# Attention weights as max(row factor, column factor) times the mask, column-grouped products in the third layer, three of its heads on GpSimd

## The chip, the cores and the metric

One core of a Trainium2 chip runs the whole program in one launch. The metric is the device time in microseconds (us) of that core, from launch to end. The engines work side by side, each through its own in-order list of instructions: TensorE (PE, its weight loads shown as PEld), VectorE (DVE), ScalarE (ACT), GpSimd (POOL), and SyncE (SP), which issues the DMAs. They meet only in semaphores. A matmul result lands in PSUM, which has eight banks of 128 x 512 fp32 here; GpSimd does not read PSUM in this kernel.

## The reference

16 graphs of 512 nodes with 128 features pass through four graph-attention layers, each with a residual and a layer norm over the features behind it. All graphs share one adjacency mask. Cut to the parts that matter:

```python
# layer 0: 4 heads, scores = q.k/sqrt(32), masked softmax, P @ v, output projection
# layer 1 (one head), layer 3b (second attention of layer 3), both with the mask:
h = x @ W;  s1 = h @ a1;  s2 = h @ a2
e = leaky_relu(s1[:, None] + s2[None, :], 0.2)          # N x N
out = softmax(where(adj > 0, e, -inf), -1) @ h
# layer 2: 8 heads of 16 features, same scores per head, plus beta*log(prior+eps), mask, softmax
# layer 3: relu(x @ mlp1) -> attention of 256 features without a mask -> elu, residual
#          -> relu(@ mlp2) -> attention of 128 features with the mask -> elu, residual
```

A score depends on one number of the row i and one of the column j. Up to a factor that depends on the row alone and cancels in the softmax, exp(leaky_relu(s + d)) is max(exp(d), exp(0.2 d) * exp(-0.8 s)), with d the target's and s the source's term.

## The kernel before, in words

The program is written out by hand as stages. `STAGES` (line 27) gives a letter to each stage of each engine and `ORDER` (line 47) is, for each engine, a string of pairs (letter, graph in hex): the exact order in which the engine issues its stages. It is software-pipelined: while graph 7 is in layer 0, graph 6 is in layer 1, graph 5 in layers 1 and 2 and graph 4 in layers 2 and 3. After about graph 3 the strings repeat with one period per graph. `BANK_OF_USE` (line 156) names the PSUM bank of every PE stage; `wrote(stage, g, k)` waits until PE has filled that use of a bank, `took` until its reader has emptied it, and `sig` waits on a named signal. P = 128 partitions, C = 4 chunks of 128 nodes; every weight matrix is held transposed, source j on the partitions (4 chunks) and target i along 512 columns. All of it is fp32 unless said. One fp32 matmul shows as two instructions, one fp32 transpose as one.

**Layer 0** (`l0_*`). Per graph: 16 score matmuls with 32 rows each, four of them on four row groups at once (L479); DVE adds the mask and takes the row maximum (L993); ACT takes the exponential (L731); PE transposes the 128 x 512 probabilities, 64 transposes (L487), ACT copies them back (L741); PE multiplies by v in four column groups of 32, 128 columns each (L498).

**Layers 1, 3 and 3b** (`gat`, names l1, l3, l3b). DVE computes dd, the target term less its maximum (L1077), ACT makes b = exp(dd) and g = exp(0.2 dd) (L766, L767). PE spreads the source term over all partitions with four transposes of a broadcast column (L545), DVE brings it to SBUF with a cap (L1087, tile R, 128 x 512), ACT exponentiates it there (L773), DVE makes P = max(R * g, b) in four instructions (L1100), and in l1 and l3b POOL multiplies each by the mask in place (L1309). PE multiplies P by [h, 1] (L556 for l1 and l3b, L640 for l3), which gives numerator and denominator.

**Layer 2** (l2). Instead of P it builds a 0/1 matrix per head. PE spreads the head's source term (`l2_s`, L580: 4 transposes a head, 8 heads), DVE compares it with -d and multiplies by the mask, 4 instructions a head, bf16 out (`l2_signs`, L1170, tile B, two buffers). POOL builds G, both branches of h times their target factors (L1337, L1339), ACT rounds it to bf16 (L804) and POOL splits the rest in two further bf16 pieces (L1347, L1350, L1355), so that three bf16 products (102 columns) carry the fp32 value. PE: `l2_v` (L592, 16 matmuls a head) and `l2_md` (L605, the unsplit mask times the second branch, 48 matmuls). ACT copies each product out (L810, tile EV, and L818, tile MD), POOL adds the three pieces (L1363, L1367, tile U) and combines the branches (L1386, L1374, L1388), DVE takes the reciprocal (L1179), POOL divides (L1396, tile O).

**Norms.** In each layer DVE takes the statistics (L1037, L1047), POOL the power -1/2 in four short instructions (L1279 to L1294), ACT applies it (L781). POOL also adds the output bias (L1271), the residual of layer 1 (L1303) and takes min(v, 0) for the elus (L1315).

## Time and profile before

| | |
|---|---|
| median of 3 runs | 1220.33 us (1213.86 to 1223.62) |
| the profiled execution's own time | 1216.26 us |
| its span in the profile | 1214.5 us |
| mean granted TensorE clock | 0.968 of 2.4 GHz |
| PE busy | 1077.1 us (89%) |
| PEld busy | 884.0 us (73%) |
| DVE busy | 969.3 us (80%) |
| ACT busy | 835.3 us (69%) |
| POOL busy | 730.7 us (60%) |

Page part 2, the span in 40 slices, a digit being tenths of busy time:

```profile
PE   2889989899999999999999999999999978788662
DVE  3467898978898889889889888898888887967432
ACT  1788788686878787878787787878787554534431
POOL 0024566566577575858667685758485869566412
PEclk9999999999999999999999999999999989979886
```

The first slice loads and prepares the weights; from the sixth on the strings repeat; the last six or seven are the drain, in which fewer and fewer graphs are left to overlap. A busy time of PE counts each matmul from its start to its modelled end, so consecutive matmuls overlap, and a gap shorter than that overlap does not show as idle. The spacing between the starts of two rows in the timeline shows what a run of instructions really takes.

### The profile page before, as it was taken

What the parts mean: (1) busy time and instruction counts of PE and PEld (TensorE: products, weight loads), DVE (VectorE), ACT (ScalarE), POOL (GpSimd) and SP (SyncE); (2) the same over time, 40 slices, a digit from 0 to 9 for tenths busy, and PEclk for the clock granted to TensorE, in tenths of its full rate; (3) what the DMA queues carried; (4) which work ended last, traced back from release to release, by engine and by line L of the source; (5) the groups of instructions that cost most, each with busy time, mean ns of one, the idle gap of its engine ahead of it and who ended that gap; (6) DMA issues with size and microseconds to landing.
All of it is one profiled execution on the core that took longest, in us unless ns stands there. A gap on an engine that the chain in (4) does not pass through costs nothing. (4 is left out here: it accounts for less than half of the span.)

```text
span 1214.5 us, 30981 instructions
## 1 busy us (share of the span) xinstructions
PE 1077.1 (89%) x10997; PEld 884.0 (73%) x10997; DVE 969.3 (80%) x2482; ACT 835.3 (69%) x2045; POOL 730.7 (60%) x991
## 2 busy tenths in 40 slices
PE   2889989899999999999999999999999978788662
PEld 1566868787878787787878888887878867667452
DVE  3467898978898889889889888898888887967432
ACT  1788788686878787878787787878787554534431
POOL 0024566566577575858667685758485869566412
PEclk9999999999999999999999999999999989979886
DMA  4000000000000000000000000000000000000000
GB/s 112 2 10 11 11 11 2 10 2 1 11 11 10 11 10 11 10 11 10 11 11 7 7 8 11 11 10 11 11 2 11 1 10 1 10 1 10 10 9 9
DMA packets 9510, 13.24 MB, mean 11 GB/s; under 512 B 2704, under 2 KB 5008, under 8 KB 9232
## 3 DMA queue, kind: packets, MB, share of 16 engines
q1 hardware_dynamic: 9360, 11.28, 3.0%
q8 instruction: 90, 1.47, 0.5%
q14 instruction: 60, 0.49, 0.1%
HBM read 7.08 MB, written 4.19 MB: 9 GB/s over the span
## 5 line engine op out<-in xcount | busy, mean ns | idle before, releaser
L1170 DVE SCALAR_TENSOR_TENSOR B<-bank,neg_d,mask_t 128x512 bf16<-128x512 f32 x512 | 346.7, 738 | 6.1 <-PE bank L580 6.1
L993 DVE CUSTOM_DVE_ANT_0 probs<-bank,mask_add 128x512 f32<-128x512 f32 x256 | 169.8, 682 | 47.7 <-PE bank L479 47.5
L731 ACT ACTIVATE probs<-probs,neg_max 128x512 f32<-128x512 f32 x256 | 183.2, 718 | 14.6 <-DVE neg_max L1001 14.6
L741 ACT ACTIVATE probs_t<-bank 128x512 f32<-128x512 f32 x256 | 148.5, 596 | 24.2 <-PE bank L487 21.2
L487 PE MATMUL bank<-ident,probs 128*128 128x128 f32 x1024 | 145.4, 277 | 16.6 <-ACT probs_t L741 7.7
L1363 POOL TENSOR_TENSOR U<-EV 128x136 f32<-128x136 f32 x128 | 57.8, 451 | 167.8 <-ACT EV L810 166.2
L487 PEld LDWEIGHTS bank<-ident,probs 128*128 128x128 f32 x1024 | 112.7, 141 | 38.7 <-ACT probs L731 19.6
L640 PE MATMUL bank<-t,l_P 128*128 128x257 f32 x512 | 123.8, 395 | 11.1 <-DVE l_P L1100 11.0
L592 PEld LDWEIGHTS bank<-GS,B 128*128 128x128 bf16 x2048 | 105.8, 98 | 24.6 <-issue 15.0
L640 PEld LDWEIGHTS bank<-t,l_P 128*128 128x128 f32 x512 | 96.8, 196 | 35.4 <-DVE l_P L1100 14.1
L592 PE MATMUL bank<-GS,B 128*128 128x102 bf16 x2048 | 115.0, 209 | 3.3 <-issue 2.0
L781 ACT ACTIVATE x<-x,shift_l,rstd_l 128x128 f32<-128x128 f32 x256 | 105.0, 482 | 17.0 <-POOL shift_l L1294 16.1
L1100 DVE TENSOR_SCALAR l_P<-l_R,l_g,l_b 128x512 f32<-128x512 f32 x128 | 102.8, 815 | 5.3 <-ACT l_R L773 2.3
L1309 POOL TENSOR_TENSOR l3b_P<-l3b_P,mask_t 128x512 f32<-128x512 f32 x64 | 75.3, 1182 | 48.6 <-DVE l3b_P L1100 48.6
L810 ACT ACTIVATE EV<-bank 128x408 f32<-128x408 f32 x128 | 64.7, 505 | 37.2 <-PE bank L592 34.1
L1309 POOL TENSOR_TENSOR l_P<-l_P,mask_t 128x512 f32<-128x512 f32 x64 | 76.5, 1201 | 21.8 <-DVE l_P L1100 21.8
L580 PE MATMUL bank<-ident,t 128*128 128x128 f32 x512 | 78.3, 282 | 0.0
L479 PE MATMUL bank<-head_k,head_q 32*128 32x512 f32 x512 | 72.7, 638 | 2.4 <-ACT probs_t L741 2.4
L556 PE MATMUL bank<-t,l3b_P 128*128 128x129 f32 x512 | 64.0, 280 | 7.3 <-POOL l3b_P L1309 7.3
L1287 POOL TENSOR_TENSOR rstd_l<-rstd_l,neg_half 128x4 f32<-128x4 f32 x64 | 68.5, 1070 | 3.0
L498 PE MATMUL bank<-probs_t,v 128*32 128x128 f32 x2048 | 69.2, 276 | 0.0
L1367 POOL TENSOR_TENSOR U<-U,EV 128x136 f32<-128x136 f32 x128 | 65.6, 516 | 5.8
(170 smaller groups left out, 2448.3 us busy)
## 6 DMA issues: line engine op xcount, KB each, us to landing
x_in<-in_x SPq DMA_DIRECT2D x16, 256.0 KB, 2.7
out<-x SPq DMA_DIRECT2D x16, 256.0 KB, 2.0
l_P<-in_adj SPq DMA_DIRECT2D x1, 1024.0 KB, 5.0
w_fc<-in_L_gnn_W_fc SPq DMA_DIRECT2D x1, 256.0 KB, 3.2
probs_t<-in_L_gnn_a_fc SPq DMA_DIRECT2D x1, 256.0 KB, 5.9
w_cat<-in_L_gnn_W SPq DMA_DIRECT2D x2, 64.0 KB, 3.4
w3a<-in_L_gnn_mlp_w SPq DMA_DIRECT2D x1, 128.0 KB, 3.4
w3b<-in_L_gnn_mlp_w SPq DMA_DIRECT2D x1, 128.0 KB, 3.1
```

The source lines that it names most:

```text
L479: pe.matmul(ps("l0_s", g, HEADS0 * c + h)[:, :], g.of(head_q)[rows, c * P:(c + 1) * P], g.of(head_k)[rows, :], start=True, stop=True)\
L487: last = pe.transpose(ps[:, j * P:(j + 1) * P], probs[m // HEADS0 % 2][:, m % HEADS0, j * P:(j + 1) * P], ident[:, :])
L580: last = pe.transpose(ps[:, c * P:(c + 1) * P], g.of(t2)[:, c, D + h:D + h + 1].broadcast_to([P, P]), ident[:, :])
L592: last = pe.matmul(ps[:, c * w3:(c + 1) * w3], B1[h % 2][:, j, c * P:(c + 1) * P], g.of(GS)[:, j * HEADS2 + h, :, :].rearrange("p a b -> p ...
L640: last = pe.matmul(ps[:, 0:HID + 1], gat["l3"]["P"][:, j, c * P:(c + 1) * P], g.of(t3)[:, j, 2:3 + HID], start=(j == 0), stop=(j == C - 1))
L731: act.activation(e, e, ACT.Exp, bias=neg_max[:, m:m + 1], scale=SCALE0, accum_out=g.of(den0)[:, m:m + 1])\
L741: act.activation(probs_t[c % 2][:, h, :, :].rearrange("p j n -> p (j n)"), ps("l0_t", g, m)[:, :], ACT.Copy)\
L781: last = act.activation(y[:, c, :], y[:, c, :], ACT.Identity, bias=shift[n][:, c:c + 1], scale=rstd[n][:, c:c + 1])
L993: dve.tensor_tensor_reduce(probs[c % 2][:, h, :], ps("l0_s", g, m)[:, :], mask_add[:, c, :], 1.0, -3.0e38, ALU.add, ALU.max, row_max[:, m: ...
L1100: dve.tensor_scalar(q["P"][:, j, :], q["R"][:, :], q["g"][:, j:j + 1], q["b"][:, j:j + 1], ALU.mult, ALU.max).then_inc(signal[n + "_P"], 1)
L1170: last = dve.scalar_tensor_tensor(B1[h % 2][:, j, :], ps("l2_s", g, h)[:, :], g.of(neg_d)[:, j, h:h + 1], mask_t[:, j, :], ALU.is_ge, ALU. ...
L1309: pool.tensor_tensor(t, t, mask_t[:, j, :], ALU.mult).then_inc(signal[n + "_Pm"], 1)
```

## The change

In all attention layers the exponential of the source term is taken on the 128 x 4 column before it is spread, not on the 128 x 512 tile after it, so DVE reads the spread factor straight from PSUM. In l1, l3b and l2 the common factor exp(0.2 d) moves from the weights into h (one POOL multiplication per layer), so a weight is max(spread factor, exp(0.8 d)) * mask, one `scalar_tensor_tensor` on DVE, with nothing for POOL to mask. Layer 2 keeps fp32 weights (P2, five slots of 128 x 4 x 512) and drops the bf16 pieces. Its products run in two groups of four heads: each head is one column group of 32 and streams 512 columns. ACT copies a group's 128 x 512 result out, PE transposes it back (`l2_n`), DVE divides (`l2_rcp`, `l2_o`). DVE makes the weights of heads 0 to 4; those of heads 5 to 7 are made by POOL: SP writes the three heads' factors to DRAM (`l2_rows`) and reads them back broadcast to all partitions (`l2_spread`, tile far_R), POOL takes the maximum in 12 instructions (`l2_p`) and multiplies by the mask in three of 128 x 2048 (`l2_m`). Heads 4, 6 and 7 reuse slots 0, 2 and 3 of the first group; head 5 has slot 4. t2 and t4 become single buffers. All order strings and the bank string are new.

```diff
 # SP (new)
+            def l2_rows(g, k):
+                sp.wait_ge(*sig("exp2", g, 3))
+                ...
+                sp.dma_start(g.of(rows2).rearrange("h p c -> p h c"), g.of(R2)[:, DVE_HEADS2:HEADS2, :])\
+                    .then_inc(signal["rows2"], 16)
+            def l2_spread(g, k):
+                sp.wait_ge(*sig("rows2", g, 16))
+                if g.has(1):
+                    sp.wait_ge(*sig("p2_max", g, 4 * FAR_HEADS2, back=1))
+                sp.dma_start(far_R[:, :, :, :].rearrange("q h p c -> q (h p c)"),
+                             g.of(rows2)....broadcast_to([P, FAR_HEADS2 * N_NODES])).then_inc(signal["spread2"], 16)
 # PE
             def attend(n, t):
-                        pe.wait_ge(*sig(n + "_Pm", g, 4))
+                        pe.wait_ge(*took(n + "_s", g))
+                        pe.wait_ge(*sig(n + "_gh", g, 1))
             def l2_s(g, h):
-                    last = pe.transpose(ps[:, c * P:(c + 1) * P], g.of(t2)[:, c, D + h:D + h + 1].broadcast_to([P, P]), ...)
+                    last = pe.transpose(ps[:, c * P:(c + 1) * P], g.of(R2)[:, h, c:c + 1].broadcast_to([P, P]), ident[:, :])
-            def l2_v(g, h):
-                for c in range(C):
-                    for j in range(C):
-                        last = pe.matmul(ps[:, c * w3:(c + 1) * w3], B1[h % 2][:, j, c * P:(c + 1) * P],
-                                         g.of(GS)[:, j * HEADS2 + h, :, :]...)
-            def l2_md(g, k):
-                ...
+            def l2_v(g, q):
+                if q == 0:
+                    pe.wait_ge(*sig("gh2", g, 1))
+                pe.wait_ge(*took("l2_s", g, GROUP2 * q + min(GROUP2, DVE_HEADS2 - GROUP2 * q) - 1))
+                if q == 1:
+                    pe.wait_ge(*sig("p2_far", g, FAR_HEADS2))
+                for j in range(C):
+                    for h in range(GROUP2):
+                        last = pe.matmul(ps[DH0 * h:DH0 * (h + 1), :], g.of(GH)[:, j, (GROUP2 * q + h) * W2:(GROUP2 * q + h) * W2 + DH0],
+                                         P2[:, slot_of(GROUP2 * q + h), j, :], start=(j == 0), stop=(j == C - 1))
+            def l2_n(g, q):
+                pe.wait_ge(*took("l2_v", g, q))
+                for c in range(C):
+                    last = pe.transpose(ps[:, c * P:(c + 1) * P], o2_raw[:, c * P:(c + 1) * P], ident[:, :])
 # ACT
-            def exp_sources(n): ...        # Exp on R, 128 x 512
-            def l2_high(g, k): ...         # G to bf16
+                    act.activation(t["R"][:, :], t["ss"][:, :], ACT.Exp, scale=-0.8)      # 128 x 4
+            def l2_v(g, q):
+                act.activation(o2_raw[:, :], ps("l2_v", g, q)[:, :], ACT.Copy)
 # DVE
-            def source_scores(n): ...      # R <- PSUM, 128 x 512
+            def masked_weights(n):         # l1, l3b; the wait on the spread bank and n_b is at j == 0
+                    made = dve.scalar_tensor_tensor(q["P"][:, j, :], ps(n + "_s", g)[:, :], q["b"][:, j:j + 1],
+                                                    mask_t[:, j, :], ALU.max, ALU.mult)
             def weights(n, last_part):     # l3
-                    dve.tensor_scalar(q["P"][:, j, :], q["R"][:, :], q["g"][:, j:j + 1], q["b"][:, j:j + 1], ...)
+                    made = dve.tensor_scalar(q["P"][:, j, :], ps(n + "_s", g)[:, :], q["g"][:, j:j + 1], q["b"][:, j:j + 1], ...)
-            def l2_signs(g, h): ...
+            def l2_p(g, h):                # heads 0 to 4
+                if h == 0:
+                    dve.wait_ge(*sig("exp2", g, 3))
+                    if g.has(1):
+                        dve.wait_ge(*wrote("l2_v", g, 1, back=1))
+                if h == GROUP2:
+                    dve.wait_ge(*wrote("l2_v", g, 0))
+                for j in range(C):
+                    last = dve.scalar_tensor_tensor(P2[:, h % GROUP2, j, :], ps("l2_s", g, h)[:, :], g.of(t2e)[:, j, h:h + 1],
+                                                    mask_t[:, j, :], ALU.max, ALU.mult)
+            def l2_rcp(g, q): ...          # reciprocal of 128 x 16 from PSUM
+            def l2_o(g, q): ...            # 128 x 256 from PSUM times the reciprocal
 # POOL
-            def mask_weights(n): ...       # l1, l3b
-            l2_g, l2_split, l2_u, l2_w, l2_c, l2_o
+            def scale(n, t): ...           # h * exp(0.2 d), 128 x 512, for l1 and l3b
+            def l2_scale(g, k): ...        # the same for layer 2
+            def l2_p(g, n):                # n = 0..11: head 5 + n // 4, chunk n % 4
+                if n == 0:
+                    pool.wait_ge(*sig("spread2", g, 16))
+                    if g.has(1):
+                        pool.wait_ge(*wrote("l2_v", g, 1, back=1))
+                if n == 4:
+                    pool.wait_ge(*wrote("l2_v", g, 0))
+                pool.tensor_scalar(P2[:, slot_of(DVE_HEADS2 + h), j, :].rearrange("q (c p) -> q c p", c=C),
+                                   far_R[:, h, :, :].rearrange("q p c -> q c p"), g.of(t2e)[:, j, ...], None, ALU.max)
+            def l2_m(g, h):
+                pool.wait_ge(*sig("p2_max", g, C * (h + 1)))
+                pool.tensor_tensor(p, p, mask_t[:, :, :], ALU.mult)       # 128 x 2048, fp32 times bf16
```

The part of the new strings that repeats with each graph, for the graph numbers of one period. POOL: `j5 b6 s3 c6 a8 d6 k5k5k5k5 p4 y5 q4 r4 e6 k5k5k5k5 y5 k5k5k5 t3 k5 f6 y5 g6 h6 i6 u3 v3 w3 x3`, where j is `l2_scale`, k `l2_p`, y `l2_m`, e and t the two `scale`, f the residual of layer 1. On PE the first product group of a graph (`t`) comes early in the period and the second late: `t5` D3 e7 D3 x4 m6 s5 f7 E3 f7 y4y4 F3F3 f7 n6 z4z4 G3 z4z4 n6 H3 f7 e8 f7f7 g7 A4 f7 J3J3 B4 f7 e8 u5 `t5`.

## Rows read from the trace of the kernel before

**Rows 1.** SP's timeline: start us, us, engine, what; two loads of x_in.
```profile
431.19 0.33 SPq L415 DMA_DIRECT2D x_in<-in_x  x1
497.59 0.33 SPq L415 DMA_DIRECT2D x_in<-in_x  x1
```

**Rows 2.** Windows, one period and the drain: length, then PE, PEld, DVE, ACT, POOL.
```profile
407.70:474.10 66.40, 64.54 (x690) 53.72 (x688) 58.98 (x154) 51.75 (x127) 45.75 (x62) 1.00 0.03 10
...
1040.00:1214.00 174.00, 115.91 (x760) 93.14 (x758) 94.95 (x215) 68.63 (x157) 80.67 (x107) 0.82 0.02 7
```

**Rows 3.** Groups by line, PE: count, then busy us, mean ns, idle before.
```profile
L487 PE MATMUL bank<-ident,probs 128*128 128x128 f32 x1024 | 145.4, 277 | 16.6 <-ACT probs_t L741 7.7 <-ACT probs L731 6.5 <-DVE v L980 1.8
L580 PE MATMUL bank<-ident,t 128*128 128x128 f32 x512 | 78.3, 282 | 0.0
```

**Rows 4.** PE's timeline, 600 to 611 us: start, us, line, operation, count.
```profile
600.27 0.88 PE L592 MATMUL bank<-GS,B 128*128 128x102 bf16 x16
600.99 1.49 PE L487 MATMUL bank<-ident,probs 128*128 128x128 f32 x12
...
603.96 0.89 PE L592 MATMUL bank<-GS,B 128*128 128x102 bf16 x16
604.78 1.14 PE L479 MATMUL bank<-head_k,head_q 32*128 32x512 f32 x8
605.86 1.75 PE L605 MATMUL bank<-GS,mask_t 128*128 128x136 bf16 x24
607.54 1.08 PE L498 MATMUL bank<-probs_t,v 128*32 128x128 f32 x32
608.43 1.06 PE L508 MATMUL bank<-ident,rden 128*32 128x128 f32 x32
...
610.02 1.04 PE L580 MATMUL bank<-ident,t 128*128 128x128 f32 x8
610.89 0.60 PE L450 MATMUL bank<-ident,x 128*128 128x128 f32 x4
```

**Rows 5.** Groups by line, DVE.
```profile
L1170 DVE SCALAR_TENSOR_TENSOR B<-bank,neg_d,mask_t 128x512 bf16<-128x512 f32 x512 | 346.7, 738 | 6.1 <-PE bank L580 6.1
...
L1100 DVE TENSOR_SCALAR l_P<-l_R,l_g,l_b 128x512 f32<-128x512 f32 x128 | 102.8, 815 | 5.3 <-ACT l_R L773 2.3 <-issue 2.2
...
L1100 DVE TENSOR_SCALAR l3b_P<-l3b_R,l3b_g,l3b_b 128x512 f32<-128x512 f32 x64 | 53.9, 851 | 2.3 <-ACT l3b_R L773 2.3
...
L1087 DVE TENSOR_SCALAR l_R<-bank,l_ndmax 128x512 f32<-128x512 f32 x32 | 23.9, 747 | 1.8 <-issue 1.7
```

**Rows 6.** Groups by line, ACT.
```profile
L741 ACT ACTIVATE probs_t<-bank 128x512 f32<-128x512 f32 x256 | 148.5, 596 | 24.2 <-PE bank L487 21.2
L810 ACT ACTIVATE EV<-bank 128x408 f32<-128x408 f32 x128 | 64.7, 505 | 37.2 <-PE bank L592 34.1 <-POOL U L1367 1.4
```

**Rows 7.** Groups by line, POOL.
```profile
L1309 POOL TENSOR_TENSOR l_P<-l_P,mask_t 128x512 f32<-128x512 f32 x64 | 76.5, 1201 | 21.8 <-DVE l_P L1100 21.8
...
L1315 POOL TENSOR_SCALAR e<-v 128x1024 f32<-128x1024 f32 x16 | 45.2, 2826 | 17.0 <-ACT v L846 16.8
...
L1347 POOL TENSOR_TENSOR G<-G,GS 128x1088 f32<-128x1088 f32 x16 | 40.6, 2540 | 16.0 <-ACT GS L804 16.0
L1337 POOL TENSOR_TENSOR G<-t,bg 128x512 f32<-128x512 f32 x32 | 33.9, 1058 | 11.6 <-ACT R L796 11.6
...
L1315 POOL TENSOR_SCALAR e<-x 128x512 f32<-128x512 f32 x16 | 23.9, 1491 | 30.1 <-issue 30.1
```

**Rows 8.** DMA issues: size, median us from issue to landing.
```profile
probs_t<-in_L_gnn_a_fc SPq DMA_DIRECT2D x1, 256.0 KB, 5.9
```

**Rows 9.** DVE's timeline near 305 us.
```profile
304.95 1.75 DVE L1001 TENSOR_SCALAR neg_max<-row_max 128x4 f32<-128x4 f32 x1
```

**Rows 10.** POOL's timeline at the same time.
```profile
304.57 2.11 POOL L1355 TENSOR_TENSOR GS<-G,GS 128x1088 bf16<-128x1088 f32 x1
```

**Rows 11.** PE's timeline in the last 20 us: the last masked attention.
```profile
1194.37 5.43 PE L556 MATMUL bank<-t,l3b_P 128*128 128x129 f32 x32 [7.30 <-POOL l3b_P L1309]
```

568 lines of the change are left out of this document (236 added, 332 removed), and 24 rows, old and new, of tables (STAGES, stored).

## The prediction, on record before the changed kernel ran

> **What bounds the kernel now.** I read the timeline of SP first, for the length of a period: two loads of x_in lie 497.59 - 431.19 = 66.4 us apart [rows 1]. Then the windows, for the load of each engine within one such period: PE 64.5 us, DVE 59.0, ACT 51.8, POOL 45.8 [rows 2]. So PE is the fullest and DVE is close behind. The reader should not take PE's 97% at its word. A row of transposes is 277 to 282 ns long [rows 3], while in an unbroken run the next one starts after 0.109 us (8 in 610.89 - 610.02 us) or some 0.117 us (12 in 1.49 us with the overlap, 1.40 without) [rows 4], so gaps up to some 0.17 us hide under the rows. Over the whole run the same groups take 145.4 / 1024 = 0.142 and 78.3 / 512 = 0.153 us each [rows 3]. Per graph that is 64 x 0.025 + 32 x 0.044 = 3.0 us of hidden waiting in these two groups alone; with the 1.9 us of shown idle, PE has about 61.5 us of real work and 4.9 us of waiting in a period of 66.4. PE's own work bounds the steady part, and the rest is the price of four in-order engines that must meet. The drain, 174 us with PE busy 116 [rows 2], is set by chains of latency.
>
> **PE, part by part, per graph.** Removed: the 16 bf16 products of a head take 0.72 us (600.27 to 600.99) or 0.82 us (603.96 to 604.78) [rows 4], eight of them 6.2 us; the two `l2_md` stages 2 x (607.54 - 605.86) = 3.4; the spreads of three heads, 12 transposes x 0.109 = 1.3. Sum 10.9. Added: `l2_v` is 2 groups x 16 fp32 products = 64 instructions of 512 columns in four column groups. The nearest row has the same four column groups with 128 columns: 32 in 608.43 - 607.54 = 0.89 us, 0.028 each [rows 4]. Four times the columns gives 0.111 each, 7.1 us. The other near row is four row groups of 512 columns, 8 in 1.08 us, 0.135 each [rows 4], 8.6 us. I take 7.1, as it is the same kind of group and a long run has less start-up; below it I allow 6.7. The upper end is no overlap at all, 4 x 0.109 = 0.44 each, 28 us. `l2_n` adds 8 transposes, 0.9. Net 10.9 - 8.0 = **-2.9 us** (-1.4 with the row-group price).
>
> **DVE.** Removed: 346.7 / 16 = 21.7 us of sign matrices, (102.8 + 53.9) / 16 = 9.8 of weights, three R tiles x 0.747 = 2.2 [rows 5], and about 0.5 of small ones. Added: 20 + 8 masked weights at 346.7 / 512 = 0.677 us, 19.0. That row writes bf16 and the new ones fp32; both read 512 fp32 from PSUM, and the fp32 row that does is 0.747 [rows 5], so at most 2 us more. Four l3 weights at 0.747, 3.0; two divisions of 256 elements and two reciprocals, about 1.3; three small score instructions, about 1.0. Net 24.3 - 34.2 = **-9.9 us**, to about 49 us. It is not on the path of the steady part; it shortens PE's waiting.
>
> **ACT.** Removed: 64.7 / 16 = 4.0 us of EV copies [rows 6], and 3.8 for the three 512-wide exponentials, the bf16 rounding and MD. Added: two copies of 512 at 0.596 [rows 6] and small exponentials, 1.8. Net **-6.0 us**.
>
> **POOL.** Removed: eight mask products at 1.2 [rows 7], 9.5, and 23.7 for G, its splits, U, MD and O, which leaves 12.5 us. Added: 12 maxima of 512 elements. The nearest row is the `tensor_scalar` of 512 contiguous elements, 1.49 us [rows 7], 17.9 in all. The new ones read every fourth element, and no row shows that; below I go to 1.06, a two-input operation of 512 [rows 7], above to 2.83, the same operation on twice the elements [rows 7]. I take 1.49. Three mask products of 2048 elements: four times the 1.06 of L1337 is 4.2, four times the 1.20 of the mask product is 4.8 [rows 7]; I take 4.3, as a long one pays its start once, 13 in all. Three scalings at 1.06 to 1.2, 3.4. Net 34.3 - 33.2 = **+1 us**, about 47 us.
> By the Trainium skill (GPSIMD Engine Reference, sections 3.1 and 4.1) a one-input operation on GpSimd runs at roughly line rate, some 0.77 us for 512 elements. The row says 1.49. By the page POOL would fall to 38 us and the first rival below would have 5.8 us more slack; the sum would not change, and I go by the row.
>
> **Transfers and queues.** The factors take two DMAs in series. The 256 KB broadcast lands in 5.9 us [rows 8]; the new one is three times that, so I allow 5 to 10 us with the small one ahead. `l2_spread` of a graph may start once POOL has read the last factor of the graph before; between that and the first maximum the new POOL string has about 17 us of other work (mask product, two norms, min, bias, scaling). That covers it, and if the cover went the excess would fall on POOL's first maximum, head 5, which has the most slack. On SP the loads and stores queue behind them; each is needed most of a period later. Cost nothing.
>
> **The sum.** Work on PE falls to 58.6 us. Of the 4.9 us of waiting I expect about 4.0 to stay, as DVE and ACT have more room. Period 62.6, 3.8 less. From the sixth slice of the page (about 175 us) to 1040 us there are 865 / 66.4 = 13 periods: -49 us. The ramp is set by layer 0, which is unchanged: -1. In the drain each attention loses the R tile, its 512-wide exponential and the mask behind the last weight, of which one wait alone is 7.3 us [rows 11]; that is some 9 us over the last graph's three. Against it the last graph's layer 2 has 12 x 1.49 + 3 x 4.3 = 31 us on POOL, where DVE had 21.7 and POOL some 13 behind it, and waits on two DMAs: +9. Zero. From the profiled execution's own 1216 us: 1166; its time is 4 us under the median, so **1170 us**. If waiting falls to 2 us instead, the period is 60.6 and the time 1144; with the row-group price and 4.9 us of waiting, 65.0 and 1202.
>
> **Rival A, the other side: POOL stands between the two product groups.** Heads 6 and 7 reuse slots of group 0, so POOL may start them only when `l2_v` group 0 is done, and group 1 waits for them; the next graph's weights on DVE wait for group 1. In POOL's string between the two stand 8 maxima (11.9), 2 mask products (8.6), the l3b scaling (1.2) and the residual (1.3): 23.0 us. PE's string has about 26.5 us of other stages there, adding them at 0.109 us per 128 columns. Slack is 3.5 us. With a maximum of 2.0 us the slack is used up and the time is about 1185 to 1200. The change is worth nothing at 1.49 + (3.5 + 3.8) / 8 = 2.4 us, and at the upper bound of 2.83 PE waits 7.2 us a graph, the period is 69.8 and the time 1220 + 13 x 3.4 = **1264 us**. For it: the access is one that no row shows, and the slack is thin. Against: POOL's runs of 16 elements in G (L1337) cost no more than contiguous ones.
>
> **Rival B: VectorE is held up by POOL's long instructions.** A 4-element operation on DVE took 1.75 us from 304.95, until 306.70 [rows 9], while POOL's instruction ran from 304.57 to 306.68 [rows 10]: DVE waited for its end. After the change there are three such instructions of 4.3 us a graph (21% of the time) and twelve of 1.5 (29%). About 17 operations of DVE a graph are small or have two SBUF inputs. If they fall at random they wait 0.21 x 2.15 + 0.29 x 0.75 = 0.67 us each, 11 us a graph, and DVE is back at 60 us: period about 65.5, **1208 us**. Against: it already happens with POOL at 69%, and the weights of l1, l3 and l3b, which suffer most now (0.815 and 0.851 us [rows 5]), leave that port by reading PSUM.
> The Trainium skill (SBUF — State Buffer, Who interferes with whom) has this as an exclusive lock on a port pair for the whole instruction. Rows 9 and 10 agree to 0.02 us.
>
> **Rival C: the column groups don't overlap** when 512 columns stream, so the change does not do what it says on PE: 28 us in place of 7.1, the period 83.5, 1440 us. The 128-column row speaks against it.
>
> **Chances.** The forecast with its own range 1120 to 1200: 0.68, of which 0.06 is left for less than 1120. Rival A in mild form (1185 to 1215): 0.08; A in full: 0.12. B: 0.10. C: 0.02. A measurement of this kernel tells about 1% from no change: 1208 to 1232. Faster by more: 0.68, most of A mild (0.07) and half of B (0.05), 0.80. Same: the rest of these two and a little of A, 0.07. Slower: A in full and C, 0.13. For 8 in 10 I leave out the slow cases (0.13) and what lies under 1120 (0.06): 1120 to 1225.
>
> **What would show it.** SP's loads 62 to 63 us apart. `l2_v` near 0.11 us a start. L1170's successor at 0.68 us. POOL's maxima at 1.5 us and mask products at 4.2 to 4.8. PE waiting for POOL's mask product ahead of group 1 of `l2_v` would mean rival A; DVE's small operations at 0.6 us and more, rival B. The forecast fails if a maximum takes over 2 us, if the columns don't overlap, or if PE's waiting grows for another reason, such as the single buffers of t2 and t4.

## The result, and the profile after

The changed kernel takes 1260.57 us (median, 1258.8 to 1264.42) against 1218.51 us for the kernel before on the same chip: a ratio of 1.035, 95% interval 1.030 to 1.040. It is slower, and the forecast of 1170 us with a range to 1225 is wrong on both counts. The profiled execution took 1258.8 us, its span is 1257.0 us, its mean granted TensorE clock 0.943 of 2.4 GHz.

SP's timeline of the changed kernel (start us, us, engine, what) answers [rows 1]:

```profile
495.43 0.33 SPq L409 DMA_DIRECT2D x_in<-in_x  x1
...
567.30 0.33 SPq L409 DMA_DIRECT2D x_in<-in_x  x1
```

A period is now 71.9 us, where 66.4 stood and 62.6 was forecast (single periods lie between 71.4 and 71.9). The windows, one period and the last 176 us (length, then PE, PEld, DVE, ACT, POOL, granted clock), answer [rows 2]:

```profile
425.73:497.43 71.70, 65.51 (x570) 47.41 (x569) 54.87 (x144) 45.68 (x119) 52.83 (x39) 0.95 0.07 20
1081.00:1257.00 176.00, 118.27 (x650) 83.70 (x642) 86.22 (x202) 57.86 (x139) 95.94 (x68) 0.85 0.03 11
```

No engine is full. DVE and ACT fell, as they should, POOL rose by 7 us a period where 1 was forecast, and the granted clock of the steady part went from 1.00 to 0.95 while PE waited more. The groups by line (count, busy us, mean ns, idle before and its releaser) answer [rows 3, 5, 7]:

```profile
L1334 POOL TENSOR_SCALAR P<-far_R,t2e 128x512 f32<-128x512 f32 x192 | 397.2, 2090 | 25.6 <-DMA far_R<-rows 24.7
L1148 DVE SCALAR_TENSOR_TENSOR P<-bank,t2e,mask_t 128x512 f32<-128x512 f32 x320 | 216.4, 739 | 3.6 <-PE bank L587 3.6
L1342 POOL TENSOR_TENSOR P<-P,mask_t 128x2048 f32<-128x2048 f32 x48 | 195.8, 4079 | 2.0
...
L599 PE MATMUL bank<-P,GH 128*32 128x512 f32 x1024 | 123.4, 625 | 4.6 <-issue 4.6
...
L1052 DVE TENSOR_SCALAR l_dd<-t,l_ndmax 128x4 f32<-128x4 f32 x32 | 65.4, 2042 | 0.1
...
L1014 DVE BATCH_NORM_STATS2 stats_l<-x 128x6 f32<-128x128 f32 x256 | 55.5, 279 | 60.3 <-POOL x L1290 59.6
```

The maximum on GpSimd (L1334) takes 2.09 us, where the sum had 1.49. DVE's four-element l_dd (L1052) takes 2.04 us on average; its mean was 0.385 us before. And the norm's statistics (L1014) wait 59.6 us in all for GpSimd's residual (L1290). How the three meet is in the timelines of one period. GpSimd first:

```profile
604.88 4.10 POOL L1334 TENSOR_SCALAR P<-far_R,t2e 128x512 f32<-128x512 f32 x2
608.94 1.05 POOL L1296 TENSOR_TENSOR t<-t 128x512 f32<-128x512 f32 x1
609.96 2.06 POOL L1334 TENSOR_SCALAR P<-far_R,t2e 128x512 f32<-128x512 f32 x1
612.00 1.26 POOL L1290 TENSOR_TENSOR x<-x 128x512 f32<-128x512 f32 x1
613.23 4.05 POOL L1342 TENSOR_TENSOR P<-P,mask_t 128x2048 f32<-128x2048 f32 x1
```

Then DVE, ACT and PE at the same time:

```profile
613.29 0.87 DVE L1014 BATCH_NORM_STATS2 stats_l<-x 128x6 f32<-128x128 f32 x4 [3.81 <-POOL x L1290]
...
614.56 2.74 DVE L1052 TENSOR_SCALAR l_dd<-t,l_ndmax 128x4 f32<-128x4 f32 x1
617.22 0.24 DVE L1054 TENSOR_SCALAR l_ss<-t,l_ndmax 128x4 f32<-128x4 f32 x1
```
```profile
617.49 0.20 ACT L766 ACTIVATE l_R<-l_ss 128x4 f32<-128x4 f32 x1 [6.63 <-DVE l_ss L1054]
```
```profile
617.94 1.11 PE L553 MATMUL bank<-ident,l_R 128*128 128x128 f32 x4 [4.04 <-ACT l_g L768]
```

Read it backwards. PE idles 4.04 us for the factors of layer 3's first attention, the one without a mask (the trace drops the digits of names, so l_dd and l_R stand for both layer 1 and layer 3; the three-operand l_P of L1080, which is layer 3's, follows at 619.33); ACT waited 6.63 us for l_ss; DVE's l_dd before it ends at 614.56 + 2.74 = 617.30, which is when GpSimd's mask product ends, 613.23 + 4.05 = 617.28. And DVE came to l_dd late, because the statistics ahead of it waited 3.81 us for the residual, which stood behind the maxima in GpSimd's queue. Over the run PE shows 46.0 us of idle time in 13 waits for l_g at this instruction, ten of them of 4.0 to 4.1 us.

The wait has a second price, which stands in the rows that follow it. First PE's timeline, then two windows of the changed kernel, with the granted clock third from the end:

```profile
618.85 1.06 PE L496 MATMUL bank<-ident,probs 128*128 128x128 f32 x4
619.84 2.09 PE L488 MATMUL bank<-head_k,head_q 32*128 32x512 f32 x8
621.86 1.11 PE L607 MATMUL bank<-ident,o_raw 128*128 128x128 f32 x4
622.91 2.59 PE L599 MATMUL bank<-P,GH 128*32 128x512 f32 x20
```
```profile
552.00:616.50 64.50, 59.75 (x550) 44.64 (x542) 50.20 (x131) 40.86 (x104) 49.23 (x33) 1.00 0.07 22
616.70:623.40 6.70, 5.46 (x24) 3.00 (x28) 4.66 (x15) 5.31 (x16) 3.62 (x6) 0.50 0.00 1
```

The clock is full up to 616.5 us and at its lower level, 1.2 in place of 2.4 GHz, from there to 623.4; PE had been idle since 613.9. The 20 instructions from 617.94 to the start of group 1 at 622.91 take 4.97 us. In e7 below, where PE idles 1.06 us and the clock stays full, the same 20 take 2.62 us (596.48 to 599.10). So the clock takes another 2.35 us, and eight periods from 473 to 975 us have such a stretch. The prediction had no term for the clock.

### The profile page after: what moved, and what is told of

The parts are those of the page before. It is cut to its first block and busy times, and to the rows that moved or that the text cites. A ratio compares the mean times of both kernels' runs of the same rounds, so it can differ in the third digit from the quotient of the medians.

```text
span 1257.0 us, 26161 instructions
## 1 busy us (share of the span) xinstructions
PE 1065.3 (85%) x9141; PEld 772.2 (61%) x9141; DVE 889.4 (71%) x2322; ACT 742.0 (59%) x1901; POOL 853.4 (68%) x621
## 5 line engine op out<-in xcount | busy, mean ns | idle before, releaser
L1334 POOL TENSOR_SCALAR P<-far_R,t2e 128x512 f32<-128x512 f32 x192 | 397.2, 2090 | 25.6 <-DMA far_R<-rows 24.7
L1148 DVE SCALAR_TENSOR_TENSOR P<-bank,t2e,mask_t 128x512 f32<-128x512 f32 x320 | 216.4, 739 | 3.6 <-PE bank L587 3.6
L1342 POOL TENSOR_TENSOR P<-P,mask_t 128x2048 f32<-128x2048 f32 x48 | 195.8, 4079 | 2.0
L1266 POOL TENSOR_TENSOR rstd_l<-mv_l,ln_eps 128x4 f32<-128x4 f32 x64 | 16.7, 261 | 220.5 <-DVE mv_l L1024 220.5
L599 PE MATMUL bank<-P,GH 128*32 128x512 f32 x1024 | 123.4, 625 | 4.6 <-issue 4.6
L776 ACT ACTIVATE x<-x,shift_l,rstd_l 128x128 f32<-128x128 f32 x256 | 105.0, 482 | 37.3 <-POOL shift_l L1281 37.2
L1014 DVE BATCH_NORM_STATS2 stats_l<-x 128x6 f32<-128x128 f32 x256 | 55.5, 279 | 60.3 <-POOL x L1290 59.6
L488 PE MATMUL bank<-head_k,head_q 32*128 32x512 f32 x512 | 83.1, 723 | 15.2 <-DVE v L957 10.4
L599 PEld LDWEIGHTS bank<-P,GH 128*32 128x32 f32 x1024 | 31.3, 115 | 74.8 <-issue 73.3
L565 PE MATMUL bank<-t,l3b_P 128*128 128x129 f32 x512 | 63.4, 284 | 4.6 <-DVE l3b_P L1066 3.4
L507 PEld LDWEIGHTS bank<-probs_t,v 128*32 128x32 f32 x2048 | 52.7, 110 | 23.3 <-ACT probs_t L741 13.0
L553 PE MATMUL bank<-ident,l_R 128*128 128x128 f32 x128 | 24.9, 327 | 48.5 <-ACT l_g L768 46.0
```

The lines of the kernel that those rows point to most:

```text
L488: pe.matmul(ps("l0_s", g, HEADS0 * c + h)[:, :], g.of(head_q)[rows, c * P:(c + 1) * P], g.of(head_k)[rows, :], start=True, stop=True)\
L507: last = pe.matmul(ps[DH0 * h:DH0 * (h + 1), 0:P], g.of(v0)[:, j, DH0 * h:DH0 * (h + 1)], probs_t[c % 2][:, h, j, :], start=(j == 0), stop ...
L599: last = pe.matmul(ps[DH0 * h:DH0 * (h + 1), :], g.of(GH)[:, j, (GROUP2 * q + h) * W2:(GROUP2 * q + h) * W2 + DH0], P2[:, slot_of(GROUP2 * ...
L776: last = act.activation(y[:, c, :], y[:, c, :], ACT.Identity, bias=shift[n][:, c:c + 1], scale=rstd[n][:, c:c + 1])
L1148: last = dve.scalar_tensor_tensor(P2[:, h % GROUP2, j, :], ps("l2_s", g, h)[:, :], g.of(t2e)[:, j, h:h + 1], mask_t[:, j, :], ALU.max, ALU ...
L1334: pool.tensor_scalar(P2[:, slot_of(DVE_HEADS2 + h), j, :].rearrange("q (c p) -> q c p", c=C), far_R[:, h, :, :].rearrange("q p c -> q c p" ...
```

## PE's time as work and waiting

I split the whole span in one way for every trace: for each kind of PE instruction the median distance to the next start is work, what goes beyond it is waiting (a lower clock counts as waiting too). Times are in us; the maximum's column is the distance between two starts.

| kernel | span | work | waiting | period | maximum | clock, 400 to 850 us |
|---|---|---|---|---|---|---|
| before | 1214.5 | 1012 | 202 | 66.4 | none | 1.00 |
| changed | 1257.0 | 976 | 281 | 71.5 | 2.06 | 0.95 |
| e2 residual first | 1215.8 | 978 | 238 | 66.7 | 2.06 | 1.00 |
| e3 l_dd, l_ss on ACT | 1212.3 | 977 | 236 | 66.7 | 2.05 | 1.00 |
| e5 write reordered | 1213.5 | 976 | 237 | 67.7 | 1.93 | 0.99 |
| e6 360 elements | 1176.0 | 978 | 198 | 65.4 | 1.52 | 1.00 |
| e13 e5 + e2 + e3 | 1191.4 | 977 | 214 | 65.7 | 1.93 | 1.00 |

PE's work fell by 36 us, 2.2 a graph, in every version that has the new products. That figure hangs on how the split counts the first and last instruction of a stage. The parts that the change touches, each count times its median spacing, fall by 41 us, 2.6 a graph: L592 and L605 took 92 and 51 us, three heads' spreads 22, and against them stand 110 for L599 and 14 for L607. By the split the loss is 79 us of waiting, and the experiments ask what it waits for. Part of it is the clock: over the whole run 142 us lie at the lower level where 78 did (two times what is missing of the mean granted clock, times the span). At half speed at most half of the 64 us more is lost, 32 us; the eight stretches above, at 2.35 each, are 19.

## Experiments

Times are medians; each was run beside the kernel before, to which the ratio refers (95% interval).

**e1, the spread rows laid out so that GpSimd reads 512 elements side by side.**

```diff
-rows2: [FAR_HEADS2, P, C];  far_R: [P, FAR_HEADS2, P, C];  max reads far_R[:, h].rearrange("q p c -> q c p")
+rows2: [FAR_HEADS2, C, P];  far_R: [P, FAR_HEADS2, C, P];  max reads far_R[:, h]
```

> The three heads' factors lie in DRAM and in far_R as [head, chunk, node], so that each of POOL's 12 maxima reads 512 contiguous elements; nothing else changes. Theory P (POOL's string between the two product groups is too long, because a maximum over every fourth element takes 2.09 us): a maximum falls to about 1.49 us, 8 of them between the groups give 4.8 us, the period falls from 71.7 to about 67, the time from 1260 to about 1200. Theory L (a small instruction of DVE, l_dd, is held 2.7 us twice a period by POOL's mask product of 4.1 us, and that alone makes PE late): l_dd still meets a mask product, the period falls by less than 1 us, 1250. The write of 4-byte elements makes l2_rows slower under both; if that is what counts, POOL waits for far_R more than the 25 us of now.

1322.26 us, ratio 1.088 (1.083 to 1.093). The maximum did fall to 1.565 us, but the small DMA of 6 KB now writes 4-byte pieces, and what is queued behind it pays:

```profile
L1334 POOL TENSOR_SCALAR P<-far_R,t2e 128x512 f32<-128x512 f32 x192 | 297.7, 1565 | 92.8 <-DMA far_R<-rows 87.2 <-PE bank L599 5.4
...
L459 PE MATMUL bank<-ident,x_in 128*128 128x128 f32 x64 | 14.9, 376 | 83.0 <-DMA x_in<-in_x 81.4 <-DVE ln_prior L951 1.6
```

The load of x_in took a median of 11.7 us to land against 3.9. So the time misses both theories, and the run gives a price for contiguous reads and nothing on the time.

**e2, the residual moved ahead.** Only GpSimd's order: in ten of the periods the residual (f) stands ahead of the scaling (t) and of the last maximum (k) of its group.

```diff
-k k k t k f y
+k k k f t k y
```

> Only POOL's order changes: the residual of layer 1 (f) goes ahead of the l3b scaling and the fourth maximum in ten of the periods, so it is made about 3.1 us earlier. Same work on every engine. Theory P and L together (DVE waits 3.8 us for the residual, then l_dd is held by the mask product, then PE waits 4.0 us for the exponential): DVE's statistics start 3.1 us earlier, l_dd is issued before the mask product starts, PE's wait at the source spread of l3 falls to about 0.5 us, 3.3 us of 71.7 in ten periods, 1227. If instead group 1 of l2_v is what POOL's string holds up (rival A as the prediction put it), moving the residual changes nothing, 1260.

1216.11 us, ratio 0.998 (0.995 to 1.001): one 1.27 us instruction moved by 3.1 us gives back 44 us, where 33 were expected. The statistics' wait for it falls from 59.6 to 28.3 us. Layer 3's l_dd now starts before the mask product and takes 0.9 us in place of 2.7 (layer 1's is still held), so this edit takes away both the wait in the queue and, on this chain, the hold. The lower clock goes from the steady part as well.

**e3, l_dd and l_ss made by ACT** (the cap on l_ss is left out).

```diff
-dve.tensor_scalar(dd, t[:, :, 1], ndmax, None, ALU.add)
-dve.tensor_scalar(ss, t[:, :, 0], ndmax, CAP, ALU.subtract, ALU.max)
+act.activation(dd, t[:, :, 1], ACT.Identity, bias=ndmax)
+act.activation(ss, t[:, :, 0], ACT.Identity, scale=-1.0, bias=ndmax)
```

> l_dd and l_ss of the three single-head attentions are made by ACT (two Identity activations of 128 x 4 ahead of the exponentials) in place of DVE; the cap of the source score is left out. ACT gets 6 small instructions of about 0.2 us a graph. Theory L: the two holds of 2.7 us a period are gone; PE's wait of 4.0 us falls by 2.5 and the 1.0 us behind the other one goes, period about 68.5, 1218. Theory P: the hold is a symptom, as DVE would wait for POOL elsewhere; at most 1 us a period, 1248 or more.

1212.37 us, ratio 0.995 (0.993 to 0.998). The statistics still wait 59.5 us for the residual, yet 48 us come back: DVE's held instruction is as good a place to mend the chain as the residual is.

**e4, the mask product in four instructions.**

```diff
-pool.tensor_tensor(p, p, mask_t, ALU.mult)                       # 128 x 2048
+for j in range(C): pool.tensor_tensor(p[:, j], p[:, j], mask_t[:, j], ALU.mult)
```

> Each mask product of 128 x 2048 on POOL is cut in four of 128 x 512. By the rows of before a 512 one takes 1.16 us, so POOL gets 0.56 us more a head. Theory L: l_dd is held at most 1.2 us instead of 2.7, two times a period, about 2 us less after POOL's extra, 1235. Theory P: POOL's string between the groups grows by 1.1 us, the period with it, 1274.

1267.87 us, ratio 1.041 (1.036 to 1.046). l_dd falls only to 1.354 us on average, and the average hides the one that counts. Layer 1's falls to 0.7 us, with the hold moved to the l_ss behind it (1.21 us). Layer 3's, on the chain above, rises from 2.7 to 3.2 us: one from 477.97 lasts until 481.14, through the rest of one piece and two more, the last of which ends at 481.11. Four pieces take 4.50 us in place of 4.05. Cutting a long instruction didn't free VectorE; the time lies near theory P's 1274.

**e5, the reordering on the side of the write.** It isn't the same step on the other side: the read side steps 16 bytes from element to element, the write side here stores groups of four elements 512 bytes apart.

```diff
-pool.tensor_scalar(P2[..., j, :] as (c p), far_R[:, h].rearrange("q p c -> q c p"), t2e, None, ALU.max)
+pool.tensor_scalar(P2[..., j, :] as (p c), far_R[:, h], t2e, None, ALU.max)
```

> One edit on the changed kernel: GpSimd's maxima (L1334) read the spread rows in the order in which they lie in memory (512 elements side by side) and write their result with a step of 16 bytes backwards into the mask's order, where the changed kernel reads with that step and writes side by side. Same elements, same count, same transfers. Theory (the step on the read costs 0.5 us of the 2.09 us; in the run with contiguous rows the instruction took 1.565 us): if only reads pay for the step, the mean falls to about 1.57 us, a graph's maxima from 25.1 to 18.8 us, and the time to about 1190 to 1215 us, since moving one 1.25 us instruction ahead of the maxima gave 44 us. Rival (the step costs the same on either side): the mean stays at 2.0 to 2.2 us and the time at 1250 to 1270 us.

1217.04 us, ratio 0.9995 (0.996 to 1.003). The mean duration is 2.049 us, the rival's, but durations of neighbours overlap, and from start to start it is 1.93 us against 2.06. Both expectations miss: the reordering costs almost the same on either side, and the time still falls by 43 us, far more than the 12 x 0.13 us a graph. On the chain PE still idles, 28.8 us in 13 waits in place of 46.0 (2.40 us at 665.16), and the granted clock of the steady part is 0.99 in place of 0.95. In its timeline the hold of VectorE stands plainly, in both directions. DVE, then GpSimd:

```profile
700.36 5.00 DVE L1179 SCALAR_TENSOR_TENSOR v<-e,v 128x1024 f32<-128x1024 f32 x1
```
```profile
699.89 0.20 POOL L1266 TENSOR_TENSOR rstd_l<-mv_l,ln_eps 128x4 f32<-128x4 f32 x1
700.04 0.20 POOL L1267 TENSOR_TENSOR shift_l<-mv_l,neg_one 128x4 f32<-128x4 f32 x1
700.19 4.09 POOL L1342 TENSOR_TENSOR P<-P,mask_t 128x2048 f32<-128x2048 f32 x1
704.24 2.02 POOL L1274 TENSOR_TENSOR rstd_l<-rstd_l,neg_half 128x4 f32<-128x4 f32 x1
```

DVE's instruction with two SBUF inputs starts 0.17 us after the mask product and ends at 705.36, 1.08 us after the product's end at 704.28; where GpSimd makes no weights (e8) it takes 1.21 us in all. Then GpSimd's 1.04 us root, queued next, takes 2.02 us: it ends 0.90 us after DVE's.

**e6, the maximum at the price of the forecast.** 90 of each 128 elements, so that part of three heads' weights isn't computed.

```diff
-pool.tensor_scalar(P2[...] as (c p),            far_R as (c p),            t2e, None, ALU.max)
+pool.tensor_scalar(P2[...] as (c p)[..., 0:90], far_R as (c p)[..., 0:90], t2e, None, ALU.max)
```

> The changed kernel with GpSimd's maxima (L1334) cut to 90 of each 128 elements, 360 of 512; the other elements of those weights keep old values, so part of three heads' weights isn't computed. Order, waits, transfers and the strided read stay. At 2090 ns for 512 this should take 1470 to 1520 ns, which is the price that the prediction used. Theory (the failed step is the price of the maximum, which sat in the sum at 1.49 us; the rest of the sum holds): period 62.6 to 65 us, 1170 to 1205 us. Rival (the sum's other steps fail too: the residual still stands behind the maxima and the mask product still holds VectorE's l_dd for 2.7 us twice a period, about 3 us of waits on PE each period): period 66 to 67, 1210 to 1225 us.

1178.21 us, ratio 0.968 (0.963 to 0.973).

```profile
L1335 POOL TENSOR_SCALAR P<-far_R,t2e 128x360 f32<-128x360 f32 x192 | 293.8, 1550 | 29.7 <-DMA far_R<-rows 23.9 <-PE bank L599 5.6
...
L1014 DVE BATCH_NORM_STATS2 stats_l<-x 128x6 f32<-128x128 f32 x256 | 55.4, 279 | 5.3 <-POOL x L1291 4.7
...
L1052 DVE TENSOR_SCALAR l_dd<-t,l_ndmax 128x4 f32<-128x4 f32 x32 | 23.2, 725 | 0.1
```

Order, waits and transfers are those of the changed kernel. The wait for the residual goes from 59.6 to 4.7 us and l_dd from 2.04 to 0.73 us. PE's 46.0 us of idle time for l_g fall to 6.6, and the clock is 1.00 in the steady part. 83 us of waiting are gone, more than the 79 that the change had added. The time lies in the theory's range; the period, 65.4, just misses its 62.6 to 65.

**e7, e2 and e3 together.**

> The changed kernel with both single edits of earlier runs together: the residual ahead of the last maximum on GpSimd's queue, and the attention score shifts (l_dd, l_ss) on ScalarE and not on VectorE. Singly they gave 1216.1 and 1212.4 us against 1260.6 us. Theory A (two separate holds on one chain, each worth about 45 us alone): together the period falls by the sum, 71.7 to about 62.5 us, 1165 to 1175 us. Theory B (one chain: residual, statistics, l_dd, l_ss, l_R; once it is shortened by 3 us PE is held by the next thing, ScalarE's or VectorE's queue or its own work of about 59.5 us and 5 us of small waits): period 65 to 66.5, 1195 to 1212 us. Theory B is the likelier, since PE still waited 7.5 to 8.1 us a period in each of the single edits.

1212.22 us, ratio 0.996 (0.994 to 0.999), the same as e3 alone. Theory A falls: the residual and l_dd are two points of one chain. What PE then meets is GpSimd's string again, at two other points. First PE, then GpSimd:

```profile
592.83 3.81 PE L570 MATMUL bank<-t,l3b_P 128*128 128x129 f32 x32 [1.06 <-issue]
596.48 0.60 PE L558 MATMUL bank<-ident,l_R 128*128 128x128 f32 x4
...
599.10 3.64 PE L604 MATMUL bank<-P,GH 128*32 128x512 f32 x32
```
```profile
591.68 1.05 POOL L1299 TENSOR_TENSOR t<-t 128x512 f32<-128x512 f32 x1
592.70 2.07 POOL L1337 TENSOR_SCALAR P<-far_R,t2e 128x512 f32<-128x512 f32 x1
594.85 4.08 POOL L1345 TENSOR_TENSOR P<-P,mask_t 128x2048 f32<-128x2048 f32 x1
```

Layer 3b's products start 0.10 us after GpSimd's scaling for them ends (592.73), which the residual has pushed back; before them PE idles 1.06 us in nearly every period. Group 1 starts 0.17 us after the third mask product ends (598.93), in e2 and e7 alike. That is rival A's place, with no room left in it, though PE doesn't idle there yet.

**e8, all eight heads on VectorE.** The order's added entries were placed by distance alone.

```diff
-DVE_HEADS2 = 5   # GpSimd's maxima, mask products and the rows' two DMAs for the others
+DVE_HEADS2 = 8   # three more l2_s on PE and l2_p on DVE a graph
```

> The change without its third part: VectorE makes all eight heads' weights of the third layer from PSUM, three more transposed score tiles on PE a graph (3 x 0.44 us) and twelve more 0.68 us instructions on VectorE; GpSimd makes none, the rows' transfers and GpSimd's maxima and mask products are gone. The larger-of-two factors and the column groups stay. The three added uses of PE and VectorE were put into the written order by their distance to the use before and after, not tuned. Theory (the 25 us of maxima and 12 us of mask products a graph on GpSimd are what costs the time, by the residual's queue and by the shared port): VectorE rises to about 54.9 + 8.1 = 63 us a graph, PE's work to 60.7, period about 66 to 68, 1205 to 1235 us, faster than the changed kernel. Rival (the time is lost elsewhere, in the products in column groups or in the order itself): no gain, 1255 us or more.

1278.71 us, ratio 1.051 (1.046 to 1.055). l_dd takes 0.24 us and the statistics wait 2.8 us, so both holds on GpSimd's side are gone. But the added score tiles wait for a bank or for ACT:

```profile
L585 PE MATMUL bank<-ident,R 128*128 128x128 f32 x512 | 78.9, 286 | 59.2 <-DVE P L1143 29.4 <-ACT t L812 17.3 <-DVE l_P L1075 4.3
```

By its numbers the rival holds (1255 us or more); that the waits come from the untuned order is argued, not shown. Whether three heads belong on GpSimd stays open; what e8 shows is that the holds follow GpSimd's weights.

**e9, group 1 kept in the rows' own column order.** The maxima read and write side by side, the mask is read in groups of four elements 256 bytes apart (not with the step of 8 bytes that the expectation names), DVE writes head 4 with a step of 16 bytes.

```diff
+pool.tensor_scalar(P2[..., j, :], far_R[:, h] as (p c), t2e, None, ALU.max)
+pool.tensor_tensor(p as (j p c), p, mask_t.rearrange("q j (c p) -> q j p c"), ALU.mult)
+o = o2_raw[:, c::4] if q else o2_raw[:, c * P:(c + 1) * P]      # the transposes of group 1
```

> The changed kernel with the columns of product group 1 (heads 4 to 7) kept in the order in which the spread rows lie in memory: GpSimd's maxima read and write 512 elements side by side; the mask product reads the mask (bf16) with a step of 8 bytes; VectorE writes head 4 with a step of 16 bytes; the transposes after group 1 read every fourth column of o2_raw. Nothing else moves and all is computed. Theory (the price of the maximum decides): the maxima start 1.54 us apart (the contiguous ones of an earlier run did) against 2.06, 12 x 0.52 = 6.2 us a graph less on GpSimd, the same as in the run with shortened maxima (1.52 us apart, period 65.4, 1178 us); if the mask product stays at 4.1 us, 1175 to 1190 us. Rival (the step is paid wherever it is moved to): the mask product rises from 4.1 to 6 us or more, or VectorE's head 4 from 0.68 to over 1.2 us each, and the time is 1205 to 1240 us.

1265.18 us, ratio 1.040 (1.036 to 1.044). The rival holds in kind: the step is paid where it is moved to. Its numbers don't: the mask product takes 5.61 us, head 4's weights 1.14 each, both just under what it named, and the time is 25 us above its range.

```profile
L1338 POOL TENSOR_SCALAR P<-far_R,t2e 128x512 f32<-128x512 f32 x192 | 297.1, 1564 | 25.3 <-DMA far_R<-rows 24.2 <-PE bank L599 1.0
L1346 POOL TENSOR_TENSOR P<-P,mask_t 128x2048 f32<-128x2048 f32 x48 | 269.1, 5606 | 2.0
L1153 DVE SCALAR_TENSOR_TENSOR P<-bank,t2e,mask_t 128x512 f32<-128x512 f32 x320 | 237.6, 819 | 3.6 <-PE bank L587 3.6
...
L1183 DVE SCALAR_TENSOR_TENSOR v<-e,v 128x1024 f32<-128x1024 f32 x16 | 69.7, 4356 | 6.2 <-ACT e L848 6.2
```

The maxima save 12 x 0.52 = 6.2 us a graph, the mask products give 3 x 1.53 = 4.6 back, and each of them now holds DVE longer: the elu's 1.21 us instruction takes 4.36. But it takes 3.20 in e6, which is fast. Where PE pays is layer 3b's maximum (L544), 37.3 us in 12 waits: in one of them PE idles 3.75 us, behind a 128 x 4 operation of DVE that is held 4.53 us (525.83 to 530.36, the mask product ends at 530.32) and head 4's weights, 3.95 us for four. In e6 the two take 3.01 and 2.71 us.

**e10, e9 with e2 and e3.**

> The permuted order of the run before together with the residual ahead of the last maximum and the score shifts on ScalarE. The question is whether what is left of PE's waiting once the maxima are cheap (198 us in the whole run with shortened maxima, 978 us of work) still lies on the residual and on VectorE's l_dd. Theory A (it does: l_dd still took 0.7 us on average with shortened maxima, and the residual still stood behind a maximum): 10 to 25 us less than the permuted kernel alone, 1155 to 1170 us. Theory B (with cheap maxima the two holds are hidden, as they became when both were taken away together: 1212.2 against 1212.4 for one alone): within 8 us of the permuted kernel.

1255.82 us, ratio 1.032 (1.027 to 1.037), 9 us less than e9, 1 more than theory B allowed and far from A's time. PE still waits 34.4 us for layer 3b's maximum. The elu's instruction (4.58 us) and the 5.58 us mask products are still there.

**e11 and e12, two more points on the curve:** maxima of 180 and of 440 elements, edited as in e6 (45 and 110 of each 128; part of three heads' weights isn't computed).

> GpSimd's maxima cut to 45 of each 128 elements, 180 of 512 (part of three heads' weights isn't computed), everything else as in the changed kernel. 512 elements cost 2.06 us from start to start, 360 cost 1.52, so 180 should cost about 0.88: 14 us a graph less than in the changed kernel, 7.7 less than with 360. It asks whether the price of the maximum still sets the period below 1.5 us. Theory A (GpSimd's string of maxima is no longer in the loop once it is short; PE's work of 61 us less its part and the other waits are): period 64 to 65.5, 1165 to 1178 us, little less than with 360. Theory B (it stays in the loop, one for one): period 58 to 60, 1080 to 1110 us, which PE's work of about 59 us a graph nearly forbids.

> GpSimd's maxima cut to 110 of each 128 elements, 440 of 512 (part of three heads' weights isn't computed), start to start about 1.80 us by the line through 360 (1.52) and 512 (2.06). The third point on the curve of time over the price of the maximum: 1.52 gave 1178 us, 2.06 gave 1260.6, and the run with the step on the write side (1.93) gave 1217. Theory A (in proportion, the string is in the loop): (1.80 - 1.52) / 0.54 of 82 us, 1178 + 43 = 1215 to 1225 us. Theory B (a threshold between 1.93 and 2.06, where an instruction of GpSimd or VectorE falls behind the mask product): flat below it, 1180 to 1205 us.

1153.43 us, ratio 0.948 (0.944 to 0.952), and 1204.55 us, ratio 0.991 (0.989 to 0.994).

| from start to start | 0.89 | 1.52 | 1.80 | 1.93 (e5) | 2.06 us |
|---|---|---|---|---|---|
| time | 1153.4 | 1178.2 | 1204.6 | 1217.0 | 1260.6 us |
| slope to the next, us per us of price | 39 | 94 | 96 | 335 | |

If the string of 12 maxima stood wholly in the period, a microsecond of price would cost 12 x 16 = 192 us. It costs a fifth of that at the cheap end, half in the middle and far more than all of it in the last 0.13 us. There PE's idle time on the chain goes from 28.8 to 46.0 us and the time at the lower clock level from 77 to 142 us; by half of the 65 more, up to 32 of the 43.5 us can be the clock. e11 falls between its two theories (1165 to 1178 and 1080 to 1110 us), with a period of 63.4 us. e12 lies at the upper edge of theory B's range, but the curve isn't flat below it.

**e13, e5 with e2 and e3.**

> Three single edits together, all computed: the maxima's step on the write side (1.93 us from start to start, alone 1217.0 us), the residual ahead of the last maximum (alone 1216.1), the score shifts on ScalarE (alone 1212.4; the last two together 1212.2). Theory A (the steep part of the curve, 56 us between a price of 1.80 and 2.06, is these two holds; with them gone time follows the string of maxima): from 1212.2 down by 12 x 0.12 us a graph x some 13 graphs = 19 us, 1190 to 1197 us. Theory B (whatever is done, 66.7 us a graph is set by something else that all these versions share): 1207 to 1213 us.

1193.83 us, ratio 0.982 (0.978 to 0.986): theory A. With the two holds gone, the reordered write is worth 1212.2 - 1193.8 = 18 us, near the 12 x 0.12 x 13 = 19 of its own length. It computes all, but for the cap on l_ss, and is faster than both kernels, by 1.8% than the one before.

**e14, two roots of the norms ahead of the mask product.** e13 with GpSimd's order changed.

```diff
-p y q r   ...   f y g h i
+p q r y   ...   f g h i y
```

> The kernel before with two more moves on GpSimd's queue: the square roots of two layer norms (one each for the third layer and the second, L1274 and L1281 of the changed kernel) stand ahead of the 4.1 us mask product that they stood behind. In the run with both edits ScalarE waits 97 us in all for shift_l, and one such root waited from 632.5 to 636.7 us behind the mask product. Theory A (GpSimd's long instructions cost by what stands behind them in its queue, and the norms are the next): 4 us a graph come off that wait, half of it reaches PE, 15 to 30 us less than without the move, 1165 to 1180 us. Theory B (the norms have slack in the written order; PE waits elsewhere): within 5 us of the run without the move.

1200.62 us, ratio 0.987 (0.983 to 0.991), 7 us more than e13. ACT's wait for shift_l fell from 89.8 to 26.7 us and nothing came of it: a long wait in a list isn't a wait on the path. The mask product, now behind the roots, is: PE idles 1.3 us ahead of group 1 in nearly every period. The statistics' wait for the residual rose from 20.0 to 29.7 us.

**e15, e6 with e2 and e3.**

> The kernel with maxima of 360 elements (start to start 1.52 us; part of three heads' weights isn't computed), which ran in 1178.2 us, with the residual moved ahead and the score shifts on ScalarE. It asks whether the two holds cost anything at the price that the prediction took. Theory A (they are holds of their own): 10 to 20 us less, 1158 to 1168 us. Theory B (at 1.52 us they are hidden, and they cost only because the maximum is dear: one failed step, the price, stands for all): within 6 us of 1178.

1167.42 us, ratio 0.960 (0.956 to 0.963), 11 us less than e6, at the near edge of theory A: at the forecast's price the holds still cost a little, and the dear maximum makes 48 us of them.

## Why the prediction was wrong

**The step that failed** is the price of GpSimd's maximum, "I take 1.49". It measured 2.09 us, 2.06 from start to start. With the price set to 1.52 and nothing else touched (e6) the time is 1178 us, 8 from the forecast and 82 from what the changed kernel takes. Two lines of the prediction could have said so. The evidence against, G's runs of 16 elements that "cost no more than contiguous ones", was a two-input operation. And 1.49 was the low part of bounds that ran to 2.83. By the Trainium skill (GPSIMD Engine Reference, section 7, Performance pitfalls for Q7 kernels) a read with a step over 8 bytes costs about half as much again, which makes 2.2 us of 1.49 as an estimate; the traces show 1.54 to 2.06, 34% more. The prediction looked up the line rate on that page and not this row.

**Two more terms of the sum were off.** "Of the 4.9 us of waiting I expect about 4.0 to stay" is one: with the price right (e6) the period is 65.4 us, and less 59 us of work (61.5 less 2.2 to 2.6) that leaves about 6 of waiting. Even maxima at 0.89 us (e11) give 63.4, above the 62.6 of the forecast; no run reached it. What makes up these 2 us is open. The other is the clock, which no term held: in the changed kernel it makes a 4.04 us wait cost 6.4 us.

**Rival A** had the right resource and, for this kernel, the wrong place, and its price curve was too flat. It put 1185 to 1200 us at 2.0 us and no gain up to 2.4; the change lost 42 us at 2.06. It looked only at group 1 of l2_v waiting for the third mask product. That had room: the product ended at 617.28, and PE began group 1 at 622.91. Part of that room was PE's own delay: once the chain is mended (e2, e7) 0.17 us are left, and in e14 PE idles there. What was late was the residual behind the same maxima, which the prediction counted as 1.3 us of GpSimd's string and never followed to the statistics, l_dd and layer 3's first attention behind it.

**Rival B** was right as a mechanism and too small alone: 1208 us. It averaged over random meetings, and in a period that repeats they aren't random. 20 of the 32 l_dd took over 2.5 us (the mean is 2.04), among them all from the eighth to the twenty-sixth, and layer 3's stand where PE waits. The Trainium skill (SBUF — State Buffer, Who interferes with whom) calls it an exclusive lock; 617.30 against 617.28 us, and the ladder in e5's timeline, agree.

**A and B are not alternatives.** e2 takes away the wait in the queue and with it the hold of layer 3's l_dd; e3 takes away the hold alone. Each gives 44 to 48 us; both give 48. They stand in series on one chain: maxima, residual, statistics, l_dd, l_ss, l_R, layer 3's spread and products. Being late in the queue is what makes layer 3's l_dd meet the mask product (2.7 us against 0.9 in e2). Both edits also bring the clock back, and at a maximum of 2.06 us both then end at a period of 66.7 us.

**PE's terms.** The column groups overlap: 32 starts from 584.42 to 588.00, where the next stage starts, are 0.112 us each, against 0.111 forecast; rival C is out. Work fell by 2.2 to 2.6 us a graph, not 2.9, which is 5 to 11 us in all.

**DVE, ACT and POOL's mask product.** The masked weights came as forecast (216.4 / 320 = 0.676 us each against 0.677), the mask product nearly (4.08 us against 4.3), and ACT's busy time fell by 93 us, 5.8 a graph against 6.0. DVE's fell by 80 us, 5.0 a graph and not 9.9: 58 us of the difference are l_dd and l3b_dd, which the holds lengthened. None of it shortened PE's waiting, as the sum had hoped.

**The near hit of e6 is partly luck.** The forecast was a period of 62.6 us and nothing from the ends. e6 has 65.4, 1.0 less than before, which is 13 us over 13 periods, where its span is 38.5 us shorter. Most of what it gained lies at the start: the last layer's first min(x, 0) on GpSimd begins at 303.11 us before, at 267.43 changed and at 249.26 in e6. From there to the end before took 1214.5 - 303.1 = 911 us and e6 took 927. By then GpSimd has added the bias of seven graphs' x_in before, of six in the other two. The first store of a result starts at 336.2 us before, at 280.8 changed and at 266.2 in e6. So the order written for the change has a graph less under way, with a shorter fill and a longer drain, and the sum saw neither.

**Transfers** were forecast at nothing. GpSimd waits 24.7 us in all for far_R, some 1.5 a graph, in a string where time is short. No run took this away alone.

## What to carry to other kernels

When work is moved to an in-order engine, price it with a row of the same operand kinds and the same step, and if there is none, let the dear bound decide whether the plan still works. Then list what is queued behind it on that engine and follow each item, not only the consumer of the moved work, to where another engine waits. Where that engine is TensorE, read the granted clock behind the wait too. A cost in series with a near-critical chain is not linear: here the same 0.26 us on an instruction cost 56 us at one end of the curve and about 10 at the other.
